# Rows of the FFN's hidden layer: rounded through int16 and transposed by DMA instead of on PE

## What is computed

```
x = x + mlstm(layernorm(x), ctx, ctx)        # 4 heads of 128, gates, a decay matrix, a normalizer, head norm
x = x + ffn(layernorm(x))
ffn(x)  = bitlinear(silu(bitlinear(x, w_gate)) * bitlinear(x, w_up), w_down)      # 512 -> 2048 -> 512
bitlinear(x, w): x is rounded to x * 127 / max|x| of its row (integers up to 127),
                 w to clip(round(w / mean|w|), -1, 1); the product is scaled back
```

## Time and profile before

| | |
|---|---|
| median of 3 runs | 656.23 us (655.87 to 660.44) |
| profiled execution, its time | 655.61 us |
| its span in the profile | 653.8 us |
| PE busy | 588.2 us (90%), 3768 instructions |
| DVE busy | 539.2 us (82%), 1427 |
| ACT busy | 467.8 us (72%), 713 |
| POOL busy | 319.1 us (49%), 487 |
| mean granted clock of PE | 0.966 |
| DMA | 63.78 MB, queue q1 27.9% of 16 engines |

### The profile page before, as it was taken

How to read it: one execution, slowest core, us unless ns; L and a number is a source line. 1 busy time by engine, 2 the same in 40 slices (tenths; PEclk the granted TensorE clock), 3 DMA queues, 4 the chain that set the end, 5 groups by cost and what they waited for, 6 DMA issues and landing times. The chain is left out here.

```text
span 653.8 us, 13097 instructions
## 1 busy us (share of the span) xinstructions
PE 588.2 (90%) x3768; PEld 387.9 (59%) x3828; DVE 539.2 (82%) x1427; ACT 467.8 (72%) x713; POOL 319.1 (49%) x487
## 2 busy tenths in 40 slices
PE   8777677798989999999999999999989997899995
PEld 7677554575646656666656655665656653465442
DVE  3376687879899898989899889989898899968762
ACT  3836977877668786779677875878677967856652
POOL 3168873455463466455556366356645455334100
PEclk9988799899999999999999999999999999999998
DMA  8697401410252122510262025212250041000001
GB/s 329 269 314 263 149 2 65 161 53 14 82 177 82 49 80 92 168 48 2 80 209 87 9 81 176 80 48 81 73 183 32 15 147 64 18 17 17 17 21 45
DMA packets 34210, 63.78 MB, mean 98 GB/s; under 512 B 2688, under 2 KB 19200, under 8 KB 31616
## 3 DMA queue, kind: packets, MB, share of 16 engines
q1 hardware_dynamic: 33600, 62.92, 27.9%
q10 hardware_dynamic: 576, 0.44, 0.3%
HBM read 54.84 MB, written 8.52 MB: 97 GB/s over the span
## 5 line engine op out<-in xcount | busy, mean ns | idle before, releaser
L647 PE MATMUL GU<-WQ,xqT 128*128 128x512 bf16 x975 | 237.8, 387 | 13.0 <-DVE FF L1457 7.1
L647 PEld LDWEIGHTS GU<-WQ,xqT 128*128 128x128 bf16 x1024 | 97.9, 99 | 114.9 <-issue 13.8
L678 PE MATMUL ACC<-WQ,FF 128*128 128x512 bf16 x501 | 116.7, 384 | 3.6 <-ACT FF L1006 1.7
L985 ACT ACTIVATE FF<-GU,cgu 128x512 f32<-128x512 f32 x128 | 86.3, 687 | 20.2 <-PE GU L647 19.3
L1457 DVE TENSOR_TENSOR FF<-FF,GU 128x512 f32<-128x512 f32 x128 | 85.3, 680 | 16.7 <-ACT FF L985 10.7
L678 PEld LDWEIGHTS ACC<-WQ,FF 128*128 128x128 bf16 x512 | 49.8, 99 | 61.0 <-ACT FF L1006 3.7
L993 ACT ACTIVATE FF<-FF,magic,hs 128x1024 f32<-128x1024 f32 x64 | 78.9, 1237 | 2.9 <-DVE hs L1488 2.9
L953 ACT ACTIVATE work<-AT,pb 128x128 f32<-128x128 f32 x128 | 47.8, 452 | 23.3 <-POOL pb L1840 22.9
L594 PE MATMUL AT<-vext,CT 128*128 128x129 f32 x256 | 50.3, 287 | 3.4 <-ACT gate_parts L891 2.1
L1862 POOL TENSOR_TENSOR work<-work,norm_bc 128x512 f32<-128x512 f32 x32 | 42.8, 1336 | 20.8 <-ACT work L953 20.8
L1826 POOL TENSOR_SCALAR pb<-den 128x4 f32<-128x4 f32 x32 | 8.1, 252 | 90.7 <-DVE den L1393 90.6
(11 more groups left out here) (126 smaller groups left out, 1211.1 us busy)
## 6 DMA issues: line engine op xcount, KB each, us to landing
bc<-gate_rows SPq DMA_DIRECT2D x32, 512.0 KB, 6.3
xin<-in_x SPq DMA_DIRECT2D x32, 256.0 KB, 3.0
kT<-in_ctx_t SPq DMA_DIRECT2D x8, 1024.0 KB, 4.9
vext<-in_ctx SPq DMA_DIRECT2D x32, 256.0 KB, 3.6
out<-FF SPq DMA_DIRECT2D x32, 256.0 KB, 2.4
WQ<-in_w_gate SPq DMA_DIRECT2D x4, 1024.0 KB, 13.1
FF<-in_w_up SPq DMA_DIRECT2D x4, 1024.0 KB, 14.6
WQ<-in_w_down SPq DMA_DIRECT2D x2, 1024.0 KB, 6.8
```

Of the source, the lines that this page charges most:

```text
L647: last = nc.tensor.matmul(dst, xqT[:, b, P * k:P * (k + 1)], w[:, k, 512 * j:512 * (j + 1)], start=(k == 0), stop=(k == KC - 1))
L678: last = nc.tensor.matmul(ACC[:, :], hT[:, b % 2, P * k:P * (k + 1)], WD[:, 4 * place(2, k // 4) + k % 4, :], start=(k == 0), stop=(k == J ...
L985: nc.scalar.activation(sg[:, j % 2, :], GU[:, 2 * (j % 2), :], ACT.Silu, scale=cgu[:, b, 0:1]).then_inc(silu_done, 1)
```

## The change

The hidden rows: round_h multiplies by hs and writes int16 (the conversion rounds), both halves packed into the front of each half of the row's own buffer. A new convert_h on DVE turns the 2048 int16 values into bf16, packed at the front of the buffer. A new turn_h on SP issues one DMA transpose [128, 2048] to hT. down on PE waits for that DMA (hT_in), and so does multiply before it writes the buffer again. transpose_h and both copy_hT are gone, and with them eight places of TP_ORDER.

The weights: weight_round writes int16(w / mean), on POOL for six quarters, on ACT for four and on DVE for two, and weight_clip on DVE clips all twelve in one instruction from int16 to bf16. Before, POOL lifted ten quarters and DVE two, and ACT took the sign of eight and DVE clipped four in two instructions each.

The orders of all five engines are new, in the opening and in the iteration, the loads of weights and x among them. keep_floor waits for the head statistics of the group before.

```diff
 TP_ORDER = [
-    ("q0", 1), ("q1", 1), ("h00", -1), ("h01", -1), ("q2", 1), ("q3", 1), ("h10", -1), ("h11", -1),
-    ("gates", 1), ("xq0", 0), ("h20", -1), ("h21", -1), ("rows", 1), ("h30", -1), ("xq1", 0),
-    ("h31", -1), ("xq2", 0), ("xq3", 0)
+    ("q0", 1), ("q1", 1), ("q2", 1), ("q3", 1), ("gates", 1), ("xq0", 0), ("rows", 1), ("xq1", 0),
+    ("xq2", 0), ("xq3", 0)
...
+        h_whole = FF[:, 0:2 * INNER].bitcast(I16).rearrange("p (r k n) -> p r k n", r=2, k=2)[:, :, :, 0:INNER // 2]
+        h_16 = FF[:, 0:2 * INNER].bitcast(BF16).rearrange("p (r n) -> p r n", r=2)[:, :, 0:INNER]
...
+            def turn_h(g, b):
+
+                if absent(g):
+                    return
+                n = g * 4 + b
+                hc_ready_at, dn_done_at = values(sp, n + 1, past("dn_done", -2) + n)
+                sp.wait_ge(hc_ready, hc_ready_at)
+                sp.sem_inc(sp_turn, 1)
+                sp.wait_ge(dn_done, dn_done_at)
+                if step_of(g) == 0 and b == 0:
+                    sp.sem_inc(sp_turn, 1)
+                    sp.wait_ge(w_whole[10], 1)
+                sp.sem_inc(sp_turn, 1)
+                sp.dma_start_transpose(hT[:, b % 2, :].rearrange("p (k t) -> p k t", t=P),
+                                       h_16[:, b % 2, :]).then_inc(hT_in[b % 2], 16)
...
                 load_x(coming, 0)
+                turn_h(oldest, 1)
+                load_x(coming, 1)
                 load_v(now, 0)
-                load_x(coming, 1)
+                store(oldest, 0)
+                turn_h(oldest, 2)
+                load_v(now, 1)
                 load_k(coming)
-                load_x(coming, 2)
-                store(oldest, 1)
-                load_v(now, 1)
                 spread_rows(now, 0)
                 spread_rows(now, 1)
+                load_v(now, 2)
+                turn_h(oldest, 3)
+                store(oldest, 1)
                 spread_rows(now, 2)
+                turn_h(former, 0)
+                store(oldest, 2)
                 spread_rows(now, 3)
-                load_x(coming, 3)
-                store(oldest, 2)
-                load_v(now, 2)
+                load_x(coming, 2)
                 load_v(now, 3)
                 store(oldest, 3)
-                store(former, 0)
+                load_x(coming, 3)
...
-            def transpose_h(g, b, half):
-                if absent(g):
-                    passed["tp"] += 1
-                    return
-                count_passed("tp", tp_out, tp_use(f"h{b}{half}", g))
-                n = g * 4 + b
-                hq_ready_at, tp_out_at = values(pe, 2 * n + (half + 1), tp_use(f"h{b}{half}", g) - 1)
-                pe.wait_ge(hq_ready, hq_ready_at)
-                if live(tp_out_at):
-                    pe.wait_ge(tp_out, tp_out_at)
-                for k in range(8):
-                    last = nc.tensor.transpose(TP16[:, P * k:P * (k + 1)], transpose_low(h[:, b % 2, :], 8 * half + k),
-                                               ident16[:, :])
-                last.then_inc(ht_done, 1)
-
             def down(g, b):
                 if absent(g):
                     return
                 n = g * 4 + b
-                tp_out_at, o_done_at = values(pe, tp_use(f"h{b}1", g), past("o_done", -1) + n)
-                if live(tp_out_at):
-                    pe.wait_ge(tp_out, tp_out_at)
+                hT_in_at, o_done_at = values(pe, g * 32 + 16 * (b // 2 + 1), past("o_done", -1) + n)
+                pe.wait_ge(hT_in[b % 2], hT_in_at)
...
-                nc.scalar.activation(h[:, b % 2, cut], h[:, b % 2, cut], ACT.Identity, bias=magic[:, 0:1],
+                nc.scalar.activation(h_whole[:, b % 2, half, :], h[:, b % 2, cut], ACT.Identity,
                                      scale=hs[:, b % 2:b % 2 + 1]).then_inc(hq_ready, 1)
...
+            def weight_round(m, c):
+
+                act.wait_ge(w_scaled, m + 1)
                 if m == 1:
-                    act.wait_ge(w_done[c // 2], 1)
+                    act.wait_ge(w_whole[c // 2], 1)
                 if m == 2 and c > 1:
-                    act.wait_ge(w_done[6 + c], 1)
-                nc.scalar.activation(ternary(m, c), staged(m, c), ACT.Sign,
-                                     bias=magic[:, 1:2]).then_inc(w_done[4 * m + c], 1)
+                    act.wait_ge(w_whole[6 + c], 1)
+                nc.scalar.activation(whole(m, c), staged(m, c), ACT.Identity,
+                                     scale=w_factor[:, m:m + 1]).then_inc(w_whole[4 * m + c], 1)
...
+                bstat_at, = values(dve, g * 4)
+                if live(bstat_at):
+                    dve.wait_ge(bstat, bstat_at)
...
+                if live(hT_in_at):
+                    dve.wait_ge(hT_in[b % 2], hT_in_at)
...
-            def copy_hT(g, b):
-
-                if absent(g):
-                    return
-                n = g * 4 + b
-                ht_done_at, dn_done_at = values(dve, past("ht_done", 0) + n * 2, past("dn_done", -2) + n)
-                dve.wait_ge(ht_done, ht_done_at)
-                dve.wait_ge(dn_done, dn_done_at)
-                if step_of(g) == 0 and b == 0:
-                    dve.wait_ge(w_done[10], 1)
-                V.tensor_scalar(hT[:, b % 2, 0:1024], TP16[:, :].bitcast(I16), -ROUND_OFFSET, None,
-                                ALU.add).then_inc(tp_out, 1)
+            def convert_h(g, b):
+
+                if absent(g):
+                    return
+                dve.wait_ge(hq_ready, g * 8 + 2 * (b + 1))
+                V.tensor_copy(h_16[:, b % 2, :].rearrange("p (k n) -> p k n", k=2), h_whole[:, b % 2, :, :]).then_inc(hc_ready, 1)
...
-            def weight_lift(m, c):
-
-                V.tensor_scalar(staged(m, c), staged(m, c), w_factor[:, m:m + 1], MAGIC, ALU.mult, ALU.add).then_inc(w_lifted[4 * m + c], 1)
+            def weight_round(m, c):
+
+                if m == 1:
+                    dve.wait_ge(w_whole[c // 2], 1)
+                if m == 2 and c > 1:
+                    dve.wait_ge(w_whole[6 + c], 1)
+                V.tensor_scalar(whole(m, c), staged(m, c), w_factor[:, m:m + 1], None, ALU.mult).then_inc(w_whole[4 * m + c], 1)
 
             def weight_clip(m, c):
 
-                dve.wait_ge(w_lifted[4 * m + c], 1)
-                if m == 1:
-                    dve.wait_ge(w_done[c // 2], 1)
-                if m == 2 and c > 1:
-                    dve.wait_ge(w_done[6 + c], 1)
-                V.tensor_scalar(ternary(m, c), staged(m, c), MAGIC, -1.0, ALU.subtract, ALU.max).then_inc(dve_seq, 1)
-                s = count.next()
-                dve.wait_ge(dve_seq, s)
-                V.tensor_scalar(ternary(m, c), ternary(m, c), 1.0, None, ALU.min).then_inc(w_done[4 * m + c], 1)
+                dve.wait_ge(w_whole[4 * m + c], 1)
+                V.tensor_scalar(ternary(m, c), whole(m, c), -1.0, 1.0, ALU.max, ALU.min).then_inc(w_done[4 * m + c], 1)
...
```

More of the change, by code:

```diff
@@ L276, in program @@
         hq_ready = sem("hq_ready")
[L277 removed]
+        hc_ready = sem("hc_ready")
+        hT_in = [sem(f"hT_in{r}") for r in range(2)]
         dn_done = sem("dn_done")
@@ L1566, in iteration @@
[L1566 to L1573 removed]
+                x1_stats(former, 0, slot_former)
+                sum_gates(now)
+                x1_scale(former, 0, slot_former)
+                head_stats(former, 1)
```

718 lines of the change are left out of this document (340 added, 378 removed), and 7 rows, old and new, of tables (OPENING_AT, OPENING_TP).

## The result

The changed kernel takes 668.80 us (median of 4 runs, 665.70 to 671.67) where the one before takes 656.40 beside it: ratio 1.0174, 95% interval 1.0116 to 1.0232. The forecast was 646.

The account below looks back on a forecast made before the run. The prediction took DVE's queue as the bound, tighter than the busier PE. Its terms, -7 for the steady state, -3 for the opening and 0 for the tail, summed to -10: 645.6 us profiled, 646 as median, range 638 to 651.

Parts of the forecast that it names:

- the steady-state term: Loop, 150 to 600 us: DVE regains two thirds of its 7.3 us of waits per 320, -7 us, bounds -10 and 0.
- a wash: Rival: transpose sometimes takes 7.5 to 8 us, or new order adds as many DVE waits as it removes; about 653, chance 0.19.
- The other operations of an iteration are the same ones in another order: DVE in the loop: apart from the copy, cast, sum and keep_floor changes, its operations stay; no cost set for reordering.
- DVE's load does not fall: DVE: loses copy_hT (32 of 688 ns), gains convert_h (32, taken at 694 ns), so its sum moves by nothing.
- The transpose, 6 us with 2.4 and 9.4 as ends: DMA transpose of 512 KB issued by SP: time to landing taken as 6 us, ends 2.4 and 9.4.
- Hidden by DVE's stretch of 7.1: DVE work between convert_h and the multiply overwriting the buffer, some 7.1 us or more, hides a 6 us transpose from DVE.
- PE's down comes well behind: PE's down needs the transposed rows late: its matching result stands some 20 us of DVE work after convert_h.
- What is queued behind a waiting turn_h [has] most of an iteration to spare: SP's queue: stores, loads of x and spreads behind a waiting turn_h each have most of an iteration to spare.
- PE's busy time down by 3.6 us an iteration: Sign in the loop: PE's busy time falls about 3.6 us an iteration while the iteration shortens by only about 1.1.
- ACT's answers more prompt: ACT loses its copy_hT, 32 of 1028 ns, 33 us, which only makes its answers to DVE prompter.
- The opening, -3 between +3 and -8: Before gate_up(0, 0, 0): POOL loses four lifts, ACT four signs, DVE's clips add 0.7 us; -3 us, between +3 and -8.
- The tail, 0 between -4 and +5: Last rows: 3.7 us more in the last row's chain against 4.5 us less PE work; net 0, between -4 and +5.

Follow-up runs that it names:

- e12: The changed kernel again, unaltered, on another chip and traced a second time: 667.67 us, ratio 1.0190 to the kernel before.
- e9: The kernel of e5 without transfer or turn_h; DVE's cast writes hT itself, transposition left out: 669.28 us, ratio 1.0212.
- e18: The kernel before with Identity in place of Silu on ACT, the FFN's activation left out: 664.85 us, ratio 1.0103.
- e11: The changed kernel with a plain DMA copy in place of each DMA transpose, transposition left out: 659.47 us, ratio 1.0077.
- e1: The changed kernel with all four gate-row spreads issued ahead of turn_h(oldest, 3) and turn_h(former, 0) in SP's queue: 664.24 us, ratio 1.0114.
- e3: The kernel before with only h's path changed (int16, DVE cast, DMA transpose), turn_h(former, 1) ahead of load_x(coming, 0): 730.21 us, ratio 1.1122.
- e5: e3 with turn_h(former, 1) made turn_h(oldest, 1) behind two loads, load_v(now, 3) moved ahead, two casts one operation later: 692.16 us, ratio 1.0439.
- e13: The changed kernel with four short filler matmuls more on PE ahead of each gate_up, 64 per iteration: 665.87 us, ratio 1.0158.
- e14: The kernel of e9 with the same filler as e13, 64 short matmuls per iteration on PE: 674.45 us, ratio 1.0289.
- e17: The changed kernel with Identity in place of Silu on ACT, the FFN's activation left out: 660.64 us, ratio 1.0049.
- e8: The changed kernel with e1, e7, opening clips moved to DVE's idle places, and norm_heads(now, 2) ahead of exp_rows(coming): 669.89 us, ratio 1.0114.
- e10: The changed kernel with no transfer and no turn_h in SP's queue; the cast writes hT, transposition left out: 664.55 us, ratio 1.0125.
- e2: The changed kernel without the transfer, transposition left out; turn_h keeps its waits on SP and only raises the semaphore: 657.57 us, ratio 0.9983.
- e7: The changed kernel with log_soft(coming) right behind exp_soft(coming) on ACT: 669.54 us, ratio 1.0106.
- e16: The changed kernel with e1, the cast moved from DVE to ACT, and opening clips in DVE's idle places: 676.53 us, ratio 1.0297.

## Why the prediction was wrong

**The step that failed is the steady-state term**, "-7 us. Bounds: -10, and 0 if the waits of the DMA take their place". It measured about +18 between group 0 and group 5 in the trace of after (4.8 to 22.7 us late, means of four rows) and +13 in e12's, and the mechanism that I allowed for the zero, multiply waiting for the DMA, did not occur. I had read that DVE sets the pace and that PE's relief is worth only what DVE stops losing, and e9 and e18 fit that: their iterations grew with DVE's busy time. From that I took two thirds of DVE's waits (7.3 us in 320) as gain, as if waits can only shrink when the other engines get lighter. e9 and e18 show the opposite on the kernel before itself: less work on PE, or on ACT, and 14 or 8 us more. My reading, which no run isolates: its 7.3 us are what is left when the order on five engines fits the arrival times; change these and the fit can go, whichever way they move. The rival "a wash" had this mechanism in half a sentence ("puts as many waits on DVE as it removes") and priced it at nothing; "The other operations of an iteration are the same ones in another order" costed the new order at nothing, and DVE stands still 3.9 us more in each iteration (3.1 in e12). Its busy share, foretold above 93%, was 86%.

**DVE's load does not fall**: right. 193.91 and 193.59 us in three iterations. convert_h at 694: 741 ns in the loop, 788 over the span, still nothing on the sum; a mean of 1212 did not occur.

**The transpose, 6 us with 2.4 and 9.4 as ends**: 4.4. **Hidden by DVE's stretch of 7.1**: right, in that multiply lost 0.2 us to it in the whole span (0.9 in e12). Hidden altogether it was not. "PE's down comes well behind" was wrong: down waited for the transpose some 1.1 us once an iteration and 12.2 us in eight places over the span, 5.4 of them before the last two rows. And e11 gains 7 to 8 us by 1.4 us less to landing and 1.5 less per issue.

**"What is queued behind a waiting turn_h [has] most of an iteration to spare"**: true of the changed kernel as laid out (e1 gains some 4 to 5 us by the ratios and not clearly, though POOL waited 50 us in 320), and wrong as a rule: in e3 a turn_h ahead of load_x, with load_v(now, 3) behind another and two casts one place earlier, costs 38 us against e5. I never looked which wait in that queue would end late.

**PE's busy time down by 3.6 us an iteration**: down by 1.0 (1.4 in e12), with a lower clock and other matmuls that took longer. I did not ask what PE's new idle time would do to its clock. By e13's ratio that is worth some 2 us, within its interval; e14 gained nothing. **ACT's answers more prompt**: no. Four copies of 1.03 us went, three table loads of 1.28 us came by the order, which I had not counted in the diff; e17, which takes ten of the twelve away, gains 7 to 9 us.

**The opening, -3 between +3 and -8**: +4.8 as the mean of the first four rows (7.5 at the first), +4.0 in e12, and gate_up at 85.61 and 83.21 instead of 73. I priced the clips by their sum on DVE ("0.7 us more") and not by where they stand: seven in a row held POOL for 4.67 us in five traces of eleven, some 2 us of gate_up's start. The rest I have not settled; the place of state_step(0, 2) ahead of gate_up is the likely cause. **The tail, 0 between -4 and +5**: about 6 us are given back over the last eight rows, and the last row's chain grew by 2.2 us where I had 3.7.

How far the loss is settled: over the loop DVE's idle time is shown to be all of it. Of some 12 us at the end, the kind of transfer (e11, 7 to 8) and the table loads (e17, 7 to 9) would each explain part. Whether they add was not run; e8 and e10 show that such parts need not. Which chain would be left when all are gone stays open. No variant beat the kernel before; e2 came level, with the transposition left out.

## What to carry to other kernels

When one queue is over 90% busy and its waits are down to 2% of the time, an edit that relieves the *other* engines has almost nothing to win and a whole fit to lose: here that cost 1 to 2%, so price a new order as a cost, not as nothing, and count the table loads per iteration in it. Look which operations with two SBUF operands on VectorE and GpSimd stand side by side before and after, and avoid a run of fast casts where GpSimd has a short step on the critical chain. Trace the same kernel twice before reading 2 us out of one trace: here its gate_up moved by 2.4 us and its iteration by 0.9. Where a wait goes into a queue shared with loads, write down for each instruction behind it when it must be out.

## What the runs showed of the hardware that was unexpected

- A 128x4 operation of GpSimd took 4.67 us for 0.19: it started 0.27 us into a run of seven VectorE clips (int16 to bf16) and ended after all seven and the operation behind them. It is not always so: in six of eleven traces with these clips it took 0.46 us, in e12 also from 0.27 us into the run, and no run shows what decides between the two.
- The contention works the other way too, and at small sizes: 16x128 operations of VectorE took 1.30 and 1.54 us for 0.28 and 0.47 beside GpSimd operations of 1.27 us.
- A DMA transpose of 512 KB within SBUF landed in 4.3 to 5.7 us (to 6.9 in e12), a plain copy of the same tile in 2.9 to 4.8 us. SP was held 1.3 to 3.3 us by one issue of the first, 0.5 to 0.6 us by one of the second.
- With 64 short matmuls fewer per iteration TensorE's granted clock in the loop was 0.96 (after) and 0.98 (e12) for 1.00 before; with 64 others put back it was 0.98. But e7 and e16, without them, had 0.99 and 1.00: that the missing matmuls alone lowered it is not shown.
